# A 12-phase decoder on one core: the first mixture routes its own tokens, the inputs load in two parts, the trees' turned tokens use four banks

## What is computed

```
# layer 0, feed-forward: three trees (q, k, v) of depth 4 choose a leaf for each token; a two-layer MLP of the leaf
for _ in range(DEPTH):
    score = einsum('nd,nd->n', xf, node_w[cur]) + node_b[cur]
    cur = 2 * cur + 1 + (score >= 0)
# layer 1, cross attention over the normed tokens and a memory, gated
logits = einsum('bsd,btd->bst', q, k) * scale            # q: normed, k: normed and memory
h_tilde = einsum('bst,bth->bsh', softmax(masked logits), v_pool)
return (1.0 - alpha) * hidden_states + alpha * h_tilde
# layer 1, feed-forward: top 2 of 8 experts, and one MLP shared by all tokens
router_probs = softmax(x @ gate_w + gate_b)
expert_values, expert_indices = top_k(router_probs, k=2)
return x + _mlp(x, sh_w1, sh_b1, sh_w2, sh_b2) + moe_out   # gelu MLPs, hidden width 512
```

## Time and profile before

| what | us |
|---|---|
| median of three executions (2467.7, 2450.97, 2447.7) | 2450.97 |
| the profiled execution, its own time | 2462.62 |
| its span from the first to the last instruction | 2460.9 |
| load, to the first attention's start | 0 to 19.5 |
| trees: first normalizing to first scatter | 409.3 to 456.7 |
| memory attention (x1) | 981.4 to 1131.5 |
| first mixture (f1), to its first expert group | 1131.5 to 1250 |

### The profile page before, as it was taken

How to read it: one execution, slowest core, us unless ns; L and a number is a source line. 1 busy time by engine, 2 the same in 40 slices (tenths; PEclk the granted TensorE clock), 3 DMA queues, 4 the chain that set the end, 5 groups by cost and what they waited for, 6 DMA issues and landing times. The chain is left out here.

```text
span 2460.9 us, 39517 instructions
## 1 busy us (share of the span) xinstructions
PE 1795.1 (73%) x14484; PEld 1224.6 (50%) x14484; DVE 1339.7 (54%) x3646; ACT 1103.6 (45%) x2273; POOL 746.4 (30%) x718
## 2 busy tenths in 40 slices
PE   3887644639877698676699668688878868852995
PEld 1554423315433365554389645365545545542774
DVE  2897497302212576555234346687439969963233
ACT  3675531213332576753144334486347757720331
POOL 1223201450242332133425400332123322246353
PEclk9888875769997799777799878699979979965997
DMA  4111361123540500210247600100000010011224
GB/s 148 83 83 83 114 218 29 48 68 86 157 115 20 200 36 3 63 35 25 88 130 237 210 1 1 35 28 10 9 3 2 2 35 21 17 40 49 71 76 138
DMA packets 143858, 173.18 MB, mean 70 GB/s; under 512 B 21041, under 2 KB 119025, under 8 KB 142737
## 3 DMA queue, kind: packets, MB, share of 16 engines
q1 hardware_dynamic: 124084, 129.09, 16.9%
q0 software_dynamic: 13248, 28.21, 3.4%
q10 hardware_dynamic: 6336, 13.37, 1.5%
HBM read 126.84 MB, written 79.05 MB: 84 GB/s over the span
## 5 line engine op out<-in xcount | busy, mean ns | idle before, releaser
L1145 PE MATMUL a_AV<-a_vx,a_pT 128*64 128x18 f32 (+1 forms) x3072 | 114.8, 223 | 32.7 <-DVE a_two L815 15.1
L1007 ACT ACTIVATE a_e<-a_e 128x512 f32<-128x512 f32 x192 | 110.2, 622 | 58.5 <-DVE a_e L837 58.3
L1145 PEld LDWEIGHTS a_AV<-a_vx,a_pT 128*64 128x64 f32 x3072 | 105.5, 146 | 61.8 <-issue 29.0
L2044 PE MATMUL f_Y<-f_h,f0w 128*128 128x512 f32 x128 | 79.3, 704 | 67.7 <-issue 39.5
L1132 PE MATMUL a_TP<-ident,a_e 128*128 128x128 f32 x768 | 108.3, 285 | 20.1 <-ACT a_e L1007 19.5
L1012 ACT COPY a_pT<-a_TP 128x512 f32<-128x512 f32 x192 | 103.5, 588 | 40.9 <-PE a_TP L1132 40.7
L1132 PEld LDWEIGHTS a_TP<-ident,a_e 128*128 128x128 f32 x768 | 89.6, 146 | 58.7 <-ACT a_e L1007 47.4
L837 DVE TENSOR_TENSOR a_e<-a_S,a_mx 128x1024 f32<-128x1024 f32 x96 | 117.2, 1221 | 2.9
L1121 PE MATMUL a_S<-a_kbd,a_qT 64*64 64x512 f32 x768 | 115.4, 677 | 1.0 <-issue 0.6
L1927 ACT ACTIVATE f_h<-f_H,f_b 128x512 f32<-128x512 f32 x64 | 44.0, 688 | 155.8 <-remote 75.1
L3592 POOL DMA_INDIRECT f_back<-f_ys,f_row x78 | 74.7, 958 | 115.5 <-DVE f_ys L3681 103.6
(11 more groups left out here) (538 smaller groups left out, 4709.6 us busy)
## 6 DMA issues: line engine op xcount, KB each, us to landing
f_wt<-in_f_ew SPq DMA_DIRECT2D x39, 584.0 KB
f_slots<-in_blank SPq DMA_DIRECT2D x1, 18576.0 KB
f_wt<-in_f_leaf SPq DMA_DIRECT2D x94, 98.0 KB
f_xs<-f_slots SPq DMA_DIRECT2D x47, 144.0 KB
memory_x_k<-w_stage ACTq DMA_DIRECT2D x24, 256.0 KB, 3.1
f_slots<-in_blank SPq DMA_DIRECT2D x1, 5760.0 KB
f_xs<-leaf_slots SPq DMA_DIRECT2D x22, 256.0 KB
leaf_out<-f_ys SPq DMA_DIRECT2D x22, 256.0 KB
```

The source lines that it names most:

```text
L1007: act.activation(eh, eh, ACT.Exp).then_inc(weights.sem, 1)
L1145: last = pe.matmul(AV[64 * c:64 * c + 64, 2 * hp * W1:2 * (hp + 1) * W1], pT[:, hp, 64 * c:64 * c + 64], vx[:, g % 2, t, c, 2 * hp:2 * hp ...
L2044: ins = pe.matmul(Y[:, :], w2[:, c, :], h[:, m % 2, :], start=False, stop=c == NC - 1)
```

## The change

The load is cut in two. SP loads 12 tiles of `x` and the columns first, and only these are waited for at the barrier; the other 20 tiles, the rows of constants and most matrices count into `k.rest_in`, for which DVE waits before the statistics of group 3 of the first attention.

In the trees, the turned tokens go over four PSUM banks (`PJ`, `Y`, two of `H`) instead of one, PE turns batch b+1 ahead of the scores of batch b, and ACT normalizes batch b+1 ahead of copying batch b.

The class `Router` and its calls are gone. The memory attention routes nothing. `routed` now has batches of eight tiles and serves f1 with its shared MLP: it routes all four batches in f1 itself, with fp32 triangle, ones and counts. Its loads (router, constants, the 584 KB of shared weights) are issued at f1's start. The old `routed`, unchanged, is now `routed_small` and serves f3; the diff writes this as an edit of `mixture`, since a diff pairs the texts that stand at the same place.

```
         def _(sp):
-            sp.dma_start(k.x[:, :, :], d["x"].rearrange("(t p) d -> p t d", p=P)).then_inc(loaded.sem, 16)
+            x = d["x"].rearrange("(t p) d -> p t d", p=P)
+            sp.dma_start(k.x[:, 0:3 * GT, :], x[:, 0:3 * GT, :]).then_inc(loaded.sem, 16)
             sp.dma_start(k.cols[:, :], d["cols"]).then_inc(loaded.sem, 16)
-            sp.dma_start(k.rows[:, :, :], d["rows"].rearrange("p (r n) -> p r n", n=P)).then_inc(loaded.sem, 16)
-            sp.wait_ge(loaded.sem, 48)
+            sp.dma_start(k.x[:, 3 * GT:NT, :], x[:, 3 * GT:NT, :]).then_inc(k.rest_in, 16)
+            sp.dma_start(k.rows[:, :, :], d["rows"].rearrange("p (r n) -> p r n", n=P)).then_inc(k.rest_in, 16)
+            sp.wait_ge(loaded.sem, 32)
 
         @block.scalar
         def _(act):
-            act.dma_start(k.mats[:, :, :], d["mats"].rearrange("p (m n) -> p m n", n=P)).then_inc(made.sem, 16)
+            mats = d["mats"].rearrange("p (m n) -> p m n", n=P)
             act.dma_start(k.ident[:, :], d["ident"]).then_inc(made.sem, 16)
+            act.dma_start(k.mats[:, 0:4, :], mats[:, 0:4, :]).then_inc(made.sem, 16)
+            act.dma_start(k.mats[:, 4:, :], mats[:, 4:, :]).then_inc(k.rest_in, 16)
             act.wait_ge(made.sem, 32)
 
-            act.wait_ge(loaded.sem, 48)
+            act.wait_ge(loaded.sem, 32)
...
-class Router:
...
             def norm_stats(n):
+                if diff and n == 3:
+                    v.wait_ge(k.rest_in, 48)
...
+    def turned(g):
+        return (PJ[:, :], Y[:, :], H[:, 0, :], H[:, 1, :])[g % 4]
...
-                act.copy(xT(g), PJ[:, :]).then_inc(xT_ready.sem, 1)
+                act.copy(xT(g), turned(g)).then_inc(xT_ready.sem, 1)
...
+            normalize(0)
             for b in range(NBAT):
-                normalize(b)
+                if b + 1 < NBAT:
+                    normalize(b + 1)
                 take_x(2 * b)
...
             def turn_x(g):
                 pe.wait_ge(xn_ready.sem, xn_ready.after(g // 2))
-                if g:
-                    pe.wait_ge(xT_ready.sem, xT_ready.after(g - 1))
-                for t in range(GT):
-                    last = pe.transpose(PJ[:, P * t:P * t + P], xn[:, GT * g + t, :], k.ident[:, :])
+                if g >= 4:
+                    pe.wait_ge(xT_ready.sem, xT_ready.after(g - 4))
+                for t in range(GT):
...
+            turn_x(0)
+            turn_x(1)
             for b in range(NBAT):
-                turn_x(2 * b)
-                turn_x(2 * b + 1)
+                if b + 1 < NBAT:
+                    turn_x(2 * b + 2)
+                    turn_x(2 * b + 3)
                 score_nodes(b)
                 if b:
...
-            r.load(sp)
-            WR = d["f1_sh"].shape[1]
-            sp.dma_start(k.f0w[:, NB * SL:NB * SL + WR], d["f1_sh"]).then_inc(k.shared_in, 16)
...
-                if g == 0:
-                    r.prepare(pool)
-                if g - 4 in (0, 2):
-                    r.root(pool, (g - 4) // 2)
-            r.scatter(pool, 0)
...
-            r.begin(v)
             for i in steps:
                 if within(i):
                     shift(i)
                 if within(i + 2):
                     norm(i + 2)
-                if i - 4 in batch:
-                    r.give_slots(v, batch[i - 4])
-                if i - 1 in batch:
-                    for j in range(4, 8):
-                        r.scale(v, batch[i - 1], j)
                 if within(i - 1):
                     take_values(i - 1)
-                if i in batch:
-                    v.wait_ge(x_updated.sem, x_updated.after(i - 1))
-                    r.norm_stats(v, batch[i])
                 if within(i + 2):
                     shift_mean(i + 2)
                 if within(i + 1):
                     bias_gate(i + 1)
                 if within(i + 2):
                     weigh_features(i + 2)
-                if i in batch:
-                    for j in range(4):
-                        r.scale(v, batch[i], j)
-                if i - 2 in batch:
-                    r.take_logits(v, batch[i - 2], no_fill)
-                if i - 3 in batch:
-                    r.make_shares(v, batch[i - 3], no_fill)
-                    r.pick(v, batch[i - 3], no_fill)
-                    r.weigh(v, batch[i - 3])
...
                 if within(i):
                     score(i)
-                if i - 4 in batch:
-                    r.place(pe, batch[i - 4])
-                if i - 2 in batch:
-                    pe.wait_ge(r.xT_ready.sem, r.xT_ready.after(batch[i - 2]))
                 if within(i - 1):
                     turn_weights(i - 1)
-                if i - 2 in batch:
-                    if batch[i - 2]:
-                        pe.wait_ge(r.places_taken.sem, r.places_taken.after(batch[i - 2] - 1))
-                    r.make_logits(pe, batch[i - 2])
...
-                if i - 1 in batch:
-                    b = batch[i - 1]
-                    for n in range(2):
-                        r.turn_x(pe, b, n, (wT_ready.sem, wT_ready.after(i - 1, n + 1)))
...
     E, F = 8, 4
     CAP = max(8, int(max(1, NB * SL * 2 // E) * 1.25))
-    BT, NBAT = 4, NT // 4
+    BT, NBAT = 8, NT // 8
...
-                if b + 3 < NBAT:
-                    root(b + 3)
+                if b == 0:
+                    root(3)
...
-def mixture(nc, k, d, tag, shared, r, store=None):
-
+def routed_small(nc, k, d, tag, shared, store=None):
...
-            r.pad(pool, payB[:, :])
-            r.root(pool, 2)
-            r.scatter(pool, 1, (0,))
-            r.root(pool, 3)
-            r.scatter(pool, 1, (1,))
-            r.scatter(pool, 2)
-            r.scatter(pool, 3)
...
-                pe.wait_ge(k.shared_in, 16)
-                do_shared(0)
-                yield_shared(0)
-                turn_batch(2)
-                r.make_logits(pe, 2)
-                do_shared(1)
-                yield_shared(1)
-                r.place(pe, 2)
-                turn_batch(3)
-                r.make_logits(pe, 3)
-                do_shared(2)
-                yield_shared(2)
-                r.place(pe, 3)
-                count_all()
-                for n in range(3, NSH):
-                    do_shared(n)
...
-        phases[4] = lambda: memory_attention(nc, k, d, "x1", ahead("f1"))
-        phases[5] = lambda: mixture(nc, k, d, "f1", shared=True, r=routers["f1"])
+        phases[4] = lambda: memory_attention(nc, k, d, "x1")
+        phases[5] = lambda: routed(nc, k, d, "f1", shared=True)
         phases[6] = lambda: pooling(nc, k, d, "a2")
         phases[8] = lambda: ternary(nc, k, d, "f2")
-        phases[11] = lambda: routed(nc, k, d, "f3", shared=False, store=out)
+        phases[11] = lambda: routed_small(nc, k, d, "f3", shared=False, store=out)
```

1070 lines of the change are left out of this document (489 added, 581 removed).

## The result

The changed kernel takes 2444.2 us (median of 20 runs), the kernel before 2460.45 us beside it (20 runs): ratio 0.9941, 95% interval 0.9927 to 0.9954. So the change takes 0.6% away, about 15 us, and between 11 and 18 by the interval. I had forecast no change.

| stretch, us | before | after | difference | I had predicted |
|---|---|---|---|---|
| start to the warping phase (w0) | 258.2 | 253.0 | -5.2 | -5.0 |
| w0 | 145.7 | 145.0 | -0.7 | 0 |
| trees (f0) | 398.4 | 392.3 | -6.1 | -3.6 |
| a1 | 179.1 | 179.2 | 0.1 | 0 |
| x1 | 150.1 | 107.9 | -42.2 | -33.6 |

What follows compares the result with a forecast made beforehand. No engine is full; each phase's last chain bounds it, broken by pauses of about 10 us under POOL's scatter runs. -5.0 - 3.6 - 33.6 + 42 = 0 on the median 2450.97: 2451 us, 8 in 10 within 2425 to 2476.

Steps and rivals of the forecast that it cites:

- The load: At the start, the barrier opens at 14.5, 5.0 us earlier, moving the attention's first root to 22.8: -5.0, between -2 and -7.
- the bound that I named but did not price: At the start, first DVE instruction waits for `a_lq`, issued behind `rows`; if it gains only 2 us, so does all.
- The trees: In the trees, four banks and a batch of lead cover PE's copy waits; last scores end sooner: -3.6, between -5.3 and 0.
- x1: Memory attention without routing loses a wait, longer steps, and the routing tail with its pause: -33.6 us, between -28 and -38.
- (a): Memory attention's start: without DVE's 4.74 us wait for `tri_all`, the statistics begin 1.9 us sooner.
- (b): Memory attention's steps: a plain step takes 12.2 us, so four steps get shorter by 2.2 each, 8.7 us.
- (c): Memory attention's tail: batch 0's picking and slots (6.3), the 10.09 us pause and PE's 6.60 us wait vanish: 23.0 us.
- f1: First mixture with all routing: rounds of 28 us, expert groups at 160 instead of 118.5: +42, between +5 and +50.
- The first: Faster rival: pauses don't follow scatters into the first mixture's loop; groups at 120 instead of 160, total 2411; chance 0.17.
- The second: Slower rival: PE stays at the low clock in the first mixture's last shared steps; +24, 2475 us; chance 0.10.
- The third: Slower rival: the start's load and the trees bring nothing; +5 to +8.6, 2456 to 2460 us; chance 0.11.
- The rule that I weighed: Instruction refills are mostly hidden in straight-line code, so PE's pauses under POOL's runs would be chance and not repeat.

## Why the prediction was wrong

**The load: right, in part by luck.** -5.0 against -5.2. The barrier opened at 12.6, not 14.5, and the bound that I named but did not price, `a_lq`, took 2.1 of the 6.9 us back. The two errors cancel, and the root came at 23.0 (22.8 predicted).

**The trees: direction right, size off.** -3.6 was forecast for the end of the last scores, where the gain was 8.4 us; -6.7 is left at the first scatter. The term that was mis-sized is PE's work, which I left at 25.6 us with four scorings of 3.65: they took 11.1 us together and not 14.6, and even before they took 13.7 (one was 2.78). The 1.8 us by which DVE's chain then held back the first scatter were not in the sum.

**x1: the steps and the pause mis-sized.** -33.6 against -42.2. A plain step lasts 11.1 us, not 12.2, and up to the last `x_nmr` the phase won 13.4 us where (a) and (b) give 10.6. (By its own numbers (b) is 4 times 2.1, 8.4 and not 8.7.) The tail behind it shrank by 28.8 (53.7 to 24.9), where I had 23.0 under (c); the pause alone costs 14.1 with its clock, by the run without the scatters, where I put 10.1. The 2.8 and the 5.8 are the 8.6 missed; 4.0 of the 5.8 are the pause, the other 1.8 I did not trace.

**f1: the step that failed.** +42 against +32.2, by "20 of live work, and I add 10 for the pause under each run less what overlaps: 28". The pause does not come on top of the live work of a round. That work is 16.2 to 17.6 us (the run without scatters), and it and the pause both lie under POOL's run of 20.2 us; only the 4.2 us that are left behind the run count, so a round is 24.4, and it stays so with bf16 places or an earlier shared step. Slots of batch 0, slots of batch 3 and first expert group were forecast 23.5, 107 and 160 us into f1 and came at 24.9, 98.8 and 149.4: the opening was 1.4 later, the three rounds 9.6 shorter, the rest behind them 2.4 shorter. (Places took PE 4.0 us, 4.5 predicted.)

**The sum.** The three parts were all forecast too dear, by 2.5, 8.6 and 9.8 us in the profiled pair, and together they are the gain that I did not see.

**The rivals.** The first (no pauses follow) did not come on the chips of the first profiles, where each full run again showed one. Its price for f1 was near: groups at 120, and they came at 118.1 without the scatters and at 121.4 on a chip without pauses. But there the kernel before loses its own pauses too, which no rival of mine had, and the change gives nothing (0.9992); that this is what I forecast is luck. The second (PE at the low clock in the last shared steps) did not come: 8.24 us a step at the full clock. The third did not come, though `a_lq` took 2.1 us.

**The rule that I weighed.** The pauses repeat where the chip has them, so they are not chance. The Trainium skill, "Runtime: NRT & Kernel Launch", section "Instruction fetch mechanics", has the cost of refilling mostly hidden in straight-line code. The pauses don't contradict that, since the trace speaks against their being waits for instructions, as one of my later expectations had it. Such a wait would have to end with a fetch that lands. But no packet of the instruction queues starts from 1113.6 to 1131.5 in the trace of after, a stretch that holds the whole pause and PE's restart at 1126.6; nor from 455 to 527 in the trees, where ACT is held five times. The fetch packets of 16 KB take as long on both kinds of chip, 1.01 and 1.11 us in the median of the changed kernel. What holds the engines stays open.

## What to carry to other kernels

A chain that crosses another engine's run is not its own work plus the stall: ask which of the two is longer, and price only what sticks out behind the longer one. When a stall is credited or charged, credit it on both sides of the comparison. A run of indirect DMAs that is cut into 8 with other work of 4 us between lets the other engines go on, but pays only where POOL has such work to do anyway: as idle filling it won 3 us of f1 on one kind of chip and lost 25 on the other. A plain DMA, where the destination is known, cost nothing on either.

## What the runs showed of the hardware

On some of the chips used (before at 2460 to 2466 us) PE, ACT and DVE come to a near stop once POOL has issued indirect DMAs for some 13 us without a break (ten or eleven of them: in f1 the run starts at 1103.19 and PE slows at 1116.6; in x1 before, 1089.02 and 1102.5); on two others (2314 to 2316 us) nothing of the kind is seen. Short breaks don't prevent it: f3, with runs of 8 and one root of about 1 us between them, is 5 to 6 us longer on the first chips, and stops of 2 us in f1 only put it off. It goes with the chip and not with the hour: one chip had it both before and after the runs on the two others. In the trees, where POOL issues 64 in 81 us, ACT then gets one activation each 14.0 us, and without pauses one each 2.23. PE had the input of the second row below ready at 503.4, 9 us before it starts. After, on a chip with pauses and on one without:

```profile
498.32 0.69 ACT L1665 ACTIVATE f_h<-f_H,f_b 128x512 f32<-128x512 f32 x1 [13.32 <-remote]
512.31 0.69 ACT L1665 ACTIVATE f_h<-f_H,f_b 128x512 f32<-128x512 f32 x1 [13.30 <-remote]
```
```profile
457.52 0.69 ACT L1665 ACTIVATE f_h<-f_H,f_b 128x512 f32<-128x512 f32 x1 [1.54 <-PE f_H L1775]
459.75 0.69 ACT L1665 ACTIVATE f_h<-f_H,f_b 128x512 f32<-128x512 f32 x1 [1.54 <-PE f_H L1775]
```

In the kernel before this makes 143 us in the three phases, 6% of its time, nine times what the change was worth. POOL's own rate is the same on both (1.26 us a scatter). What differs in the chips stays open, as does whether rests in the trees would win back their 94 us there: the run with them fell on a chip without pauses, where they cost little (300.3 us against 298.0 for the phase).
